# Moving ScalarE's sums, half units of products, a guess, doubt flags and norms in a four-layer graph kernel

## The reference

```python
def reference(x, adj, ...):
    # x: 2048 x 128, adj: 2048 x 2048, sparse, all float32
    h = relu(layernorm(x));  x = x + gcn(h, adj, W0, b0)
    h = relu(layernorm(x));  x = x + attention_layer(h, adj, ...)
    h = relu(layernorm(x));  x = x + hypergraph(h, adj, L2W)
    h = relu(layernorm(x));  x = x + hyperbolic(h, adj, L3W, b3)
    return x

def attention_layer(X, S, W1, W2, W3, U1, U2, ln_g, ln_b):
    R = (S + I) / rowsum(S + I); Z = 0; Xf = Xa = X
    for n in range(2):
        probs = softmax((Xa @ W1.T @ W2.T) @ (Xa @ W3.T).T)
        A = top_p(probs, 0.9)          # largest entries up to mass 0.9, rows renormed
        Xf = R @ Xf;  Xa = A @ Xa
        Z = Z + Xf @ U1[n].T + Xa @ U2[n].T
    return layernorm(X + Z) * ln_g + ln_b
```

## Time and profile before

| | |
|---|---|
| median of 3 timed runs | 1072.57 us (1072.1 to 1072.85) |
| profiled execution | 1073.61 us, span 1071.8 us |
| PE busy | 838.4 us (78%) |
| VectorE busy | 779.4 us (73%) |
| ScalarE busy | 509.2 us (48%) |
| POOL busy | 70.5 us (7%) |
| mean granted clock of TensorE | 0.894 of full speed |

### The profile page before, as it was taken

The page is one execution under the profiler, slowest core; times in us unless marked ns, Lnnn a source line. Parts: engine busy times, 40 slices in busy tenths (PEclk is TensorE's granted clock), DMA queues, the critical chain, the costliest instruction groups (busy, mean ns, idle before and its releaser), DMA issues.

```text
span 1071.8 us, 12286 instructions
## 1 busy us (share of the span) xinstructions
PE 838.4 (78%) x3886; PEld 563.7 (53%) x3886; DVE 779.4 (73%) x2363; ACT 509.2 (48%) x979; POOL 70.5 (7%) x68
## 2 busy tenths in 40 slices
PE   4879958887887843839778978868289899996795
PEld 4844325555655633737356557547258475553342
DVE  5978679888998998961797889789799502326715
ACT  4877235357367376314452664764765332023212
POOL 0020110000000000000000000010000200002201
PEclk9999987888988985969799789979689999998798
DMA  9949203334004000000044220220152546500001
GB/s 335 354 173 430 104 29 129 130 106 158 1 1 158 1 1 1 1 2 1 1 157 149 87 79 1 94 119 1 49 209 78 230 161 245 226 1 0 1 0 39
DMA packets 20221, 108.25 MB, mean 101 GB/s; under 512 B 1824, under 2 KB 8752, under 8 KB 9776
## 3 DMA queue, kind: packets, MB, share of 16 engines
q1 hardware_dynamic: 18752, 106.77, 26.7%
q10 hardware_dynamic: 1392, 0.61, 0.2%
HBM read 88.23 MB, written 19.14 MB: 100 GB/s over the span
## 4 chain that ended last, share of the span: by engine, by line
PE 47%; DVE 29%; ACT 11%; issue 9%; POOL 2%; DMA 1%; DVEq 1%; POOLq 0%; SPq 0%; ACTq 0%
DVE AT L1525 9%; PE PS L808 9%; PE PS L743 7%; PE PS L676 5%; PE PS L880 5%; PE PS L546 4%; DVE mxv L1664 4%; DVE nd L1528 3%; PE PS L1063 3%; PE PS L1039 3%; DVE AT L2111 2%; PE PS L1069 2%; ACT BC L1252 2%; ACT AT L1252 2%; ACT AT L1085 1%
## 5 line engine op out<-in xcount | busy, mean ns | idle before, releaser
L1085 ACT ACTIVATE AT<-PS 128x512 f32<-128x512 f32 (+2 forms) x240 | 118.2, 562 | 127.1 <-PE PS L546 107.8
L743 PE MATMUL PS<-K,ST 128*128 128x512 f32 x224 | 129.4, 731 | 15.7 <-ACT EA L1220 8.1
L546 PE MATMUL PS<-ident,AT 128*128 128x128 f32 x544 | 84.1, 289 | 42.5 <-DVE AT L1525 18.0
L1525 DVE SCALAR_TENSOR_TENSOR AT<-EA,se 128x2048 uint8<-128x2048 f32 (+1 forms) x46 | 107.6, 2345 | 1.6 <-DVE se L1518 0.3
L1525 DVE SCALAR_TENSOR_TENSOR AT<-AT 128x2048 uint8<-128x2048 f32 (+2 forms) x48 | 96.1, 2002 | 1.8 <-PE PS L546 0.8
L1664 DVE TENSOR_REDUCE mxv<-PS 128x1 f32<-128x2048 f32 x32 | 73.3, 2289 | 30.4 <-PE PS L743 24.7
L546 PEld LDWEIGHTS PS<-ident,AT 128*128 128x128 f32 x544 | 67.5, 150 | 50.9 <-DVE AT L1525 18.9
L743 PEld LDWEIGHTS PS<-K,ST 128*128 128x128 f32 x224 | 50.6, 238 | 78.1 <-issue 78.0
L2111 DVE MAX8 AT<-AT 128x8 f32<-128x256 f32 x256 | 87.6, 411 | 0.7
L808 PE MATMUL PS<-hr,AT 128*128 128x128 f32 x512 | 69.2, 284 | 8.5 <-ACT AT L1085 7.7
L808 PE MATMUL PS<-AT 128*128 128x128 f32 x512 | 67.4, 279 | 10.2 <-ACT AT L1085 9.7
(11 more groups left out here) (297 smaller groups left out, 1471.1 us busy)
## 6 DMA issues: line engine op xcount, KB each, us to landing
AT<-keep_at SPq DMA_DIRECT2D x32, 1024.0 KB, 5.1
EA<-in_adj SPq DMA_DIRECT2D x20, 1024.0 KB, 6.8
keep_at<-AT SPq DMA_DIRECT2D x8, 2048.0 KB, 24.9
AT<-keep_at SPq DMA_DIRECT2D x8, 2048.0 KB, 12.2
AT<-in_adj SPq DMA_DIRECT2D x12, 1024.0 KB, 5.7
EA<-keep_degrees SPq DMA_DIRECT2D x1, 1024.0 KB, 6.4
keep_x<-K SPq DMA_DIRECT2D x4, 256.0 KB, 8.6
out<-EA SPq DMA_DIRECT2D x4, 256.0 KB, 2.3
```

The lines of the kernel that those rows point to most:

```text
L546: return pe.transpose(dst, src, ident[0:p, 0:p])
L743: mm = pe.matmul(bank(half(gi, k) + n), ST[1][:, k * P:(k + 1) * P], wide_keys[:, n * BK:(n + 1) * BK], start=True, stop=True)
L1085: return act.activation(dst, src, ACT.Copy)
L1525: return dve.scalar_tensor_tensor(out=o, in0=x0, scalar=s, in1=x1, op0=op0, op1=op1, **k)
```

## The change

- PE: `unit_sums` is split into `unit_freed` (waits) and `unit_part(u, h)`, half a unit. In group 0 the order becomes: unit 0, logits 1, unit 1's products, logits 2, unit 1's rows, first half of unit 2, logits 3, second half and rows of unit 2, unit 3.
- ScalarE, group 0: of the six passes of the sums m = 0, four are issued one at a time: behind unit 3's copy, behind its scalings, between the two copies of `queries`, and behind them. Unit 3 follows the guess as a whole, unit 2 stands before it.
- ScalarE, `attend`: `between` (the guess, for k = 3) stands ahead of `result_out`.
- ScalarE, step 1: in group 2 `second_norm(0)` stands before the sums m = 0, `second_scaled(0)` behind the first tile of them, and `first_norm(1)` before the sums m = 1. In group 3 `first_scaled(1)` stands ahead of the loop, and rows of b = 1 are turned at k = 1, 2 and summed at k = 2, 3, one tile earlier than before.
- VectorE: `crossing_checked` stands before the wait for the mean; the fourth tile's pass is issued at once behind it, and the doubt flags are interleaved with the first threshold's arithmetic, each waiting on the instruction before the last (`v.wait(1)`).

```diff
-            def unit_sums(u):
+            def unit_freed(u):
+            def unit_part(u, h):
                 left = hr if p == 0 else Xf
-                for j in range(NT):
-                    if j % HALF == 0:
-                        pe.wait_ge(slab_in[j // HALF], 16 * (u + 1))
+                pe.wait_ge(slab_in[h], 16 * (u + 1))
+                for j in range(h * HALF, (h + 1) * HALF):
...
                         else:
+                            at = units_by(NB * step) + k
                             if k > 0:
                                 logits(step, 1, k)
-                            if k < UNITS_IN[NB * step]:
-                                unit(step, 0, units_by(NB * step) + k, True)
+                            if k == 2:
+                                unit_rows(at - 1)
+                            if k == 3:
+                                unit_part(at - 1, 1)
+                                unit_rows(at - 1)
+                            if k == 1 or k == 2:
+                                unit_begun(step, 0, at, True)
+                            if k == 1:
+                                unit_part(at, 1)
+                            if k == 0 or k == 3:
+                                unit(step, 0, at, True)
...
                     copy(stg[b % 2], bank(4 + b % 2)).then_inc(e_copied, 1)
+                    if b == 1 and between:
+                        between()
                     if b == 1 and k > 0:
                         result_out(k - 1)
-                    if b == 1 and between:
-                        between()
...
-                    if normed == 0:
-                        first_scaled(0)
-                    elif normed == 1:
-                        first_norm(1)
+                    if normed is not None:
+                        first_scaled(normed)
                     for k in range(G):
                         if g > 0:
                             attend(step, g - 1, k, ...)
-                            if normed == 1 and k == 0:
-                                first_scaled(1)
...
-                        if g == 0:
-                            if k == G - 1:
-                                guess(step, 1)
+                        if g == 0 and k != 2:
                             unit_next()
+                        if g == 0 and k == G - 1:
+                            guess(step, 1)
+                            unit_sums(u)
+                            one_below(step, 1, 0, 0, 0)
+                            unit_rows(u)
+                            u += 1
+                            one_below(step, 1, 0, 0, 1)
                     if g < NB - 2:
-                        queries(step, g + 2)
+                        queries(step, g + 2, (lambda: one_below(step, 1, 0, 1, 0)) if g == 0 else None)
+                    if g == 0:
+                        one_below(step, 1, 0, 1, 1)
                     if more:
-                        sums_below(step, g + 1, 0, (0, 1, 2))
-                        unit_next()
-                        if step == 1 and g == 1:
-                            first_norm(0)
                         if normed == 0:
                             second_norm(0)
-                            sums_below(step, g + 1, 1, (0,))
+                            sums_below(step, g + 1, 0, (0,))
                             second_scaled(0)
-                        sums_below(step, g + 1, 1, (1,) if normed == 0 else (0, 1))
+                            sums_below(step, g + 1, 0, (1, 2))
+                        else:
+                            sums_below(step, g + 1, 0, (2,) if g == 0 else (0, 1, 2))
+                        unit_next()
+                        if step == 1 and g > 0:
+                            first_norm(g - 1)
+                        sums_below(step, g + 1, 1, (0, 1))
...
+            def doubtful_with_sums(nq, n):
+                mass_above(EA if n % 2 == 0 else EB, n, G - 1)
+                v.wait(1)
+                v.put(tt(s_(3), s_(3), s_(4), ALU.max))
...
+                dve.wait_ge(sum_ok, sums_by(n, 0) + 2 * (G - 1))
+                v.put(stt(pa, below[:, 1, :], float(N), ALU.add, nq.th, ALU.mult))
+                v.wait(1)
...
+                crossing_checked(q)
                 if left > 1:
                     logit_mean(gi + 2)
-                crossing_checked(q)
-                doubtful()
-                if left > 0:
-                    last_tile(nq, gi + 1)
-                    surplus_below(nq, gi + 1, 0)
-                    last_surplus(nq)
+                if left == 0:
+                    doubtful()
+                else:
+                    doubtful_with_sums(nq, gi + 1)
                     first_step(nq)
```

More of the change, by code:

```diff
@@ L746, in logits, with unit_begun @@
                 mm.then_inc(logits_ok, 1)
-            def unit(step, g, u, early=False):
+            def unit_begun(step, g, u, early=False):
                 pe.wait_ge(mean_ok, NB * step + (2 if early else min(g + 3, NB)))
@@ L752, in unit @@
                     pe.wait_ge(z_ok, G * (NB * step + g))
-                unit_sums(u)
+                unit_freed(u)
+                unit_part(u, 0)
+            def unit(step, g, u, early=False):
+                unit_begun(step, g, u, early)
+                unit_part(u, 1)
                 unit_rows(u)
@@ L814, in attend @@
                 turns(1)
-                if normed is not None and k - normed in (1, 2):
-                    rows_turned(normed, k - normed - 1)
+                if normed is not None and k in (1, 2):
+                    rows_turned(normed, k - 1)
                 if k > 0:
@@ L821, in attend @@
                 mults(0)
-                if normed is not None and k - normed in (1, 2):
-                    pe.wait_ge(ln_ts, 2 * normed + k - normed)
-                if normed is not None and k - normed in (2, 3):
+                if normed is not None and k in (1, 2):
+                    pe.wait_ge(ln_ts, 2 * normed + k)
+                if normed is not None and k in (2, 3):
                     pe.wait_ge(exT_ok, G * gi + k)
-                    rows_summed(normed, k - normed - 2)
+                    rows_summed(normed, k - 2)
                 if k > 0:
@@ L848, in rows_turned @@
                 if b < 2:
[L849 removed]
+                    pe.wait_ge(z_ok, NT + G * (b + 1) + h)
                 for k in range(2):
@@ L1171, in _, with queries @@
             act.wait_ge(sums, NT)
-            def queries(step, g):
+            def queries(step, g, between=None):
                 gi = NB * step + g
@@ L1177, in queries @@
                 copy(ST[0][0:DA, :], bank(7)[0:DA, :]).then_inc(t1_out, 1)
+                if between:
+                    between()
                 act.wait_ge(q_mm, gi + 1)
@@ L1239, in sums_below, with one_below @@
             def sums_below(step, g, m, tiles):
+                for k in tiles:
+                    for f in range(2):
+                        one_below(step, g, m, k, f)
+            def one_below(step, g, m, k, f):
                 gi = NB * step + g
@@ L1244, in sums_below @@
                 th = guesses[g % 2][:, 0, :]
-                n = sums_by(gi, m)
                 act.wait_ge(th_ok, thresholds_by(gi, m) + 1)
-                n += 2 * tiles[0] if g > 0 else 0
-                for k in tiles:
-                    for f, func in enumerate((ACT.Relu, ACT.Sign)):
-                        if n > 1:
-                            act.wait_ge(sum_ok, n - 1)
-                        act.activation(act_junk[f], E[:, k, :], func, scale=-1.0, bias=th[:, k:k + 1],
-                                       accum_out=below[:, f, k:k + 1]).then_inc(sum_ok, 1)
-                        n += 1
+                n = sums_by(gi, m) + f + (2 * k if g > 0 else 0)
+                if n > 1:
+                    act.wait_ge(sum_ok, n - 1)
+                act.activation(act_junk[f], E[:, k, :], ACT.Relu if f == 0 else ACT.Sign, scale=-1.0,
+                               bias=th[:, k:k + 1], accum_out=below[:, f, k:k + 1]).then_inc(sum_ok, 1)
             def attend(step, g, k, between=None, normed=None, inside=None):
@@ L1263, in result_out @@
                     copy(dst, bank(7)[:, 0:P]).then_inc(exT_ok, 1)
-                    if normed is not None and k - normed in (0, 1):
-                        turned_out(normed, k - normed)
+                    if normed is not None and k < 2:
+                        turned_out(normed, k)
                     act.wait_ge(z_mm, c + 1)
@@ L1272, in result_out @@
                            .then_inc(z_ok, 1)
-                    if normed is not None and k - normed in (1, 2):
-                        summed_out(normed, k - normed - 1)
+                    if normed is not None and k in (1, 2):
+                        summed_out(normed, k - 1)
                 c = G * gi + k
```

28 lines of the change are left out of this document (22 added, 6 removed).

## The result

The changed kernel takes 1081.28 us (median of 4 executions, 1079.57 to 1083.13) against 1072.71 for the kernel before (4 executions): a ratio of 1.008, interval 1.006 to 1.010. It is 8.6 us slower, outside my range (1067.5 to 1078.5). The profiled executions are 1082.18 and 1073.61 us, their spans 1080.4 and 1071.8.

The account below looks back on a forecast made before the run. No engine was taken to bound the kernel alone (matrix products 47% of the chain, VectorE 29%, ScalarE 11%). Terms 3.0 + 1.1 + 1.4 + 1.4 + (1.4 - 0.6) - 6.8 = +0.9 on 1072.57 gave 1073.5 us, range 1067.5 to 1078.5.

Parts of the forecast that it names:

- The guess ahead of the result's copy: Last tile of group 1 of both steps and group 2 of step 0: projection late, +1.4 each, bounds 0 to 1.6.
- the first group's bound: Step 0's first group, upper bound 4.5: TensorE also drops to half clock, its logits taking 1 to 1.5 us more.
- the 1.2 us for eight cold transposes: Step 1, group 2: after nine idle microseconds PE's eight transposes run at half the clock, +1.2.
- First group of step 0: Unit 3 later and ScalarE's passes delay queries, logits, units 4 and 5 and group 2's exponential: +3.0, bounds 1.5 to 4.5.
- The third, 0.48: Step 0's first group: ScalarE's third early pass, before q_out where it waited 1.51 us, makes the chain 0.48 late.
- First group of step 1: Only the first early pass sticks out (1.2), unit 3's copy no longer waits for the guess (0.1): +1.1, bounds 0 to 2.
- The flags: Doubt flags interleaved with the sums' steps on VectorE: -0.6 in group 2 of step 0, nothing elsewhere.
- Step 1, group 2 and after: Adjacency products run under VectorE's work, the attention starts earlier and later PE waits go: -6.8, bounds -9.5 to -3.
- The last wait: Tail of step 1: POOL's root takes 1.01 us instead of 3.00, so PE's wait of 2.71 goes: -2.7.
- A: Slower rival, tail of step 1: POOL's last root meets VectorE's masks; with the first group's upper bound, 1077.7 us; chance 0.22.
- B: Faster rival: the guess finds its gap ready, so all three delays of 1.4 go; 1068.8 us; chance 0.15.
- C: Faster rival: ScalarE's early passes in the first groups hide, as PE's queries are slower; 1069.4 us; chance 0.15.

Follow-up runs that it names:

- e10: The changed kernel with eight needless transposes put into TensorE's wait for the late copy of the transposed result; 1077.82 us, 1.0059.
- e1: The changed kernel with the guess put back behind ScalarE's copy of the transposed result; 1075.35 us, 1.0019 of the kernel before.
- e2: The changed kernel with ScalarE's four early passes of the first groups put back behind the queries, unit 2 still split; 1078.7 us, 1.0059.
- e14: The kernel before with only the doubt flags between the sums' steps, the mean left ahead of the cut check; 1070.96 us, 0.9988.
- e11: The kernel before with the norms' new places and the doubt flags between the sums' steps, the mean left ahead of the cut check; 1069.57 us, 0.9973.
- e7: The kernel before with only the places of the norms changed; 1068.78 us, 0.9968.
- e13: The changed kernel with the guess between ScalarE's two copies, two early passes ahead of unit 3's copy and two behind the queries; 1066.04 us, 0.9941.
- e16: As e13, but with VectorE's mean left ahead of the cut check; 1067.2 us, 0.9953 of the kernel before.
- e3: The changed kernel with the guess between ScalarE's copies of the transposed and the projected result; 1075.0 us, 1.0019 of the kernel before.
- e4: The kernel before with only the guess moved ahead of the copy of the transposed result; 1082.66 us, 1.0096.
- e6: The kernel before with only the doubt flags between the sums' steps and the mean moved behind the cut check; 1072.72 us, 1.0008.

## Why the prediction was wrong

**The guess ahead of the result's copy: mechanism right, size wrong, and the largest miss.** I had ScalarE early, the gap late, the projection 1.4 us late in three places, 4.2 in all, with 1.6 as the upper bound of each. Putting it back takes 7.1 us out of the traces (3.93 to 0.34, 2.64 to -0.82) and 5.9 out of the medians; made alone it costs 9.5. The step that failed is "1.4 late, with PE's later transposes behind it": I charged the wait and not the work behind it. In group 1 of step 0 the wait itself came to 1.2 us, near my 1.4, and the lower clock of the products behind it to 1.7 more (3.70 us in place of 2.00). e10 shows it with the place's length kept. The three places cost 2.9, 0.7 and 3.5 against e1: in the second the clock is down in e1 as well. I had used just this effect in the first group's bound and in the 1.2 us for eight cold transposes, and left it out here.

**First group of step 0: 3.0 predicted, 5.3 measured.** The terms were 0.3 for the split and 2.7 for the passes. "Unit 3 is started some 0.3 us later" failed: it is 1.8 us later (219.95 against 216.62, less 1.55), and 2.1 at its end. I moved the fourth logits and forgot that ScalarE's copy of unit 2 then comes behind the fourth exponential. The first two passes did what I said: TensorE waits 1.3 and 0.6 us longer (2.22 and 1.31 against 0.88 and 0.68; predicted 1.46 and 0.76). The third, 0.48, doesn't show. The lower clock adds 0.5 on L709 and 0.7 on the logits, which I had as this term's upper bound. These make 5.3 in all (2.13, 1.34, 0.63, 0.53 and 0.68). Against e2 the passes read as 3.9 (5.34 less 1.47), because in e2 the same products run at the upper clock, which they don't in the kernel before.

**First group of step 1: 1.1 predicted, 0.9 measured, and right by accident.** The split gains 2.5 to 3.0 there, by the clock, and the passes cost 3.4 (0.87 less -2.52). I had expected neither.

**The flags** were to save 0.6 in group 2 of step 0, as part of the guess's delay; alone, in e14, they show -0.1 there and -0.4 in group 1, less than such a stretch varies by from trace to trace. Their -2.5 in the end was in no term of mine. It lies at TensorE's wait of 21.88 us: the products behind it start 2.1 us earlier in e14. The norms' new place takes that wait away, and with both (e11) the flags add nothing.

**Step 1, group 2 and after: -6.8 predicted, -5.7 measured, by another split.** Down to the products at 842.33 my terms give -4.4, and the changed kernel shows -4.3 (842.33 less its 14.33 until there, against 832.35), as do the norms alone (e7). Then these products take 5.10 us in place of 3.67 (6.72 in e7), which my 1.2 for the transposes didn't cover. The last wait gives back 1.8, not 2.7. And 1.0 lies in the last layer, in 64 products that the change doesn't touch (29.58 us in place of 30.54): luck.

**The rivals.** A, the last root beside VectorE's masks, came in a small form: the root took 1.01 us, but the multiply behind it met the first mask, 1.85 against its usual 0.20, and TensorE's wait of 0.91 hangs on it. My margin of 1.3 us between norm and masks was 0.8 (856.73 for POOL's first instruction, 857.53 for the mask). B and C were wrong. C names the right cure, though: passes that hide do gain, but in the 6.93 us wait ahead of unit 3's copy (e13), where I never looked for room, and not behind it. The kernel before has no such wait; the split and the earlier guess make it. The case that came, lateness that is paid again in the clock, I had as a bound of one term and not as a rival.

## What to carry to other kernels

When an instruction is put in front of a copy that TensorE waits for, charge the wait and then the work behind it at half clock; here that made over twice the wait in two of three places, and nothing more where the clock was down already. If extra work must go on a helper engine near a critical chain, look for the helper's longest wait on that chain and put it ahead of the copy that ends the wait, up to what fits (two passes of four), and not behind it. A part's effect must be read with the others: the mean's move made TensorE wait 2.70 us beside the flags alone and cost nothing in e16 against e13, and the flags' gain was gone once the norms had moved. And a stretch of one trace must not be trusted below some 2 us where the clock changes level in it, as the same code shows both levels. The version that follows from the runs, e13, is 0.6% faster than the kernel before and 1.4% faster than the changed one (1066.04 against 1081.28).

## What the runs showed of the hardware

Behind a wait of 1.07 us on TensorE products ran at half the clock (0.79 for two products of 0.39; granted clock 0.91 over 20 us), and eight needless transposes in it kept the clock up (1.00) and made the kernel 3.5 us faster. The wait of 2.15 us that ends 1.2 us ahead of it was there in both. An equal wait does not always do it. The wait of 2.15 us in the last tile of group 2, step 0, leaves the clock up in the kernel before and drops it in e1 and e3, where the products behind it take 1.9 us and not 1.06:

```profile
386.88 1.16 PE L813 MATMUL PS<-hr,AT 128*128 128x128 f32 x8 [2.15 <-ACT AT L1097]
...
389.68 1.91 PE L813 MATMUL PS<-hr,AT 128*128 128x128 f32 x8
```
```profile
381.26 1.16 PE L808 MATMUL PS<-hr,AT 128*128 128x128 f32 x8 [2.15 <-ACT AT L1085]
...
383.36 1.06 PE L808 MATMUL PS<-hr,AT 128*128 128x128 f32 x8
```

The first is e1, the second the kernel before; in e1 and e3 group 1 is 1.5 and 1.6 us faster than before, in e1 through the means (1.05 us in place of 1.49) and the logits (5.38 in place of 6.59) at its end, so the drop was shifted from one group to the next. The Trainium skill (TensorE: Matmul & The Clock Gate, "What's actually happening") says that the chip's watch over TensorE's activity runs free and isn't aligned with the kernel, so that the same work may fall on either side. These rows agree with it, and so do the 1.43 and 1.07 us of the same products behind the same waits in the kernel before and in e4, e6 and e7. But no run here moved a kernel as a whole against the watch, so that stays open, as does how much of the run-to-run spread (1069.0 to 1075.5 for the kernel before) comes from it.
